# Another fill order with zero products at time zero, conversions in mid-beat, and the reciprocals' row ahead of two loads

## The reference

```python
q, k, v = split(xn @ w_qkv)           # 16 heads of 32
q, k = rope(rmsnorm(q) * gamma_q), rope(rmsnorm(k) * gamma_k)
s = softmax(causal(q @ k.T / sqrt(32))) @ v @ w_out
W = (wq - 128) * scale                 # integer weights, hidden size 1408
g = silu((silu(xn @ Wg.T) * (xn @ Wu.T)) @ Wd.T)
out = x + s * g
```

## Time and profile before

| what | value |
|---|---|
| time, median of 3 runs | 697.89 us (697.45 to 701.13) |
| the profiled execution: its own time, its span | 698.82 us, 697.1 us |
| TensorE busy | 654.9 us, 94% of the span |
| VectorE busy | 540.3 us, 78% |
| ScalarE busy | 456.6 us, 65% |
| GpSimd busy | 413.1 us, 59% |
| DMA moved | 94.40 MB, mean 135 GB/s |

### The profile page before, as it was taken

How to read it: one execution, slowest core, us unless ns; L and a number is a source line. 1 busy time by engine, 2 the same in 40 slices (tenths; PEclk the granted TensorE clock), 3 DMA queues, 4 the chain that set the end, 5 groups by cost and what they waited for, 6 DMA issues and landing times.

```text
span 697.1 us, 12559 instructions
## 1 busy us (share of the span) xinstructions
PE 654.9 (94%) x3690; PEld 552.2 (79%) x3690; DVE 540.3 (78%) x1345; ACT 456.6 (65%) x1010; POOL 413.1 (59%) x590
## 2 busy tenths in 40 slices
PE   5988998999999999899999998999999979969997
PEld 4877887888888888788888887888878866747886
DVE  4795788898787879988878799969786797556584
ACT  2778776787676667876765678766757686633441
POOL 4987676687566657785656678757665583510000
PEclk9999999999999999999999999999999999998999
DMA  7525444414434332144342322244442514479883
GB/s 269 205 106 188 146 154 152 153 36 133 126 104 122 108 96 74 46 138 122 108 123 77 103 78 65 77 132 117 127 137 93 176 52 129 121 219 308 273 318 107
DMA packets 62531, 94.40 MB, mean 135 GB/s; under 512 B 12032, under 2 KB 24320, under 8 KB 62336
## 3 DMA queue, kind: packets, MB, share of 16 engines
q1 hardware_dynamic: 62464, 93.59, 44.0%
HBM read 59.09 MB, written 25.82 MB: 122 GB/s over the span
## 4 chain that ended last, share of the span: by engine, by line
PE 59%; POOL 14%; DVE 8%; issue 7%; DMA 6%; ACT 3%; SPq 2%; DVEq 0%; POOLq 0%; ACTq 0%
PE bank L1405 17%; PE bank L1302 12%; PE bank L1381 7%; PE bank L1342 6%; POOL rr L601 4%; PE bank L1363 4%; PE bank L1431 4%; PE bank L1430 4%; PE bank L1327 3%; PE bank L1314 3%; POOL pp L621 3%; POOL rb L610 2%; POOL ra L607 2%; DMA wd_raw<-w_down 2%; DVE pp L1028 2%
## 5 line engine op out<-in xcount | busy, mean ns | idle before, releaser
L621 POOL TENSOR_SCALAR_AFFINE_SELECT pp<-pp 128x256 fp32r<-128x256 f32 x256 | 110.2, 443 | 145.5 <-DVE pp L1028 145.2
L1050 DVE CUSTOM_DVE_ANT_0 bank<-bank,msk_w 128x128 f32<-128x128 f32 (+3 forms) x256 | 121.1, 509 | 39.3 <-PE bank L1363 39.1
L1028 DVE TENSOR_TENSOR pp<-pf,pp 128x512 fp32r<-128x512 f32 (+1 forms) x192 | 134.8, 702 | 5.8 <-ACT pp L750 5.6
L601 POOL TENSOR_TENSOR rr<-ss,half 128x8 f32<-128x8 f32 x64 | 108.4, 1695 | 24.8 <-DVE ss L996 24.6
L1302 PE MATMUL bank<-wq,xnt_h 128*128 128x384 f32 x512 | 111.9, 340 | 7.2 <-DVE qn L1008 6.8
L749 ACT ACTIVATE pf<-bank 128x512 f32<-128x512 f32 (+1 forms) x192 | 100.6, 524 | 25.6 <-PE bank L1327 23.0
L1405 PE MATMUL bank<-xnt_h,wgu 128*128 128x512 f32 x352 | 98.7, 402 | 7.5 <-DVE g L1078 4.9
L1342 PE MATMUL bank<-pp,va 128*65 128x512 f32 (+3 forms) x512 | 98.1, 310 | 3.3 <-POOL pp L621 3.3
L750 ACT ACTIVATE pp<-bank 128x512 fp32r<-128x512 f32 (+1 forms) x192 | 101.0, 526 | 0.0
L1302 PEld LDWEIGHTS bank<-wq,xnt_h 128*128 128x128 f32 x512 | 88.5, 188 | 11.2 <-issue 8.9
L1405 PE MATMUL bank<-xnt_l,wgu 128*128 128x512 f32 x352 | 96.5, 396 | 0.0
(11 more groups left out here) (83 smaller groups left out, 1187.2 us busy)
## 6 DMA issues: line engine op xcount, KB each, us to landing
wgu<-wg_dram SPq DMA_DIRECT2D x66, 256.0 KB, 3.1
hf_dram<-g SPq DMA_DIRECT2D x44, 256.0 KB, 3.3
hf_raw<-hf_dram SPq DMA_DIRECT2D x16, 512.0 KB, 6.8
wg_dram<-wgu SPq DMA_DIRECT2D x22, 256.0 KB, 3.2
xr<-x SPq DMA_DIRECT2D x16, 256.0 KB, 4.3
oh<-oraw SPq DMA_DIRECT2D x64, 64.0 KB, 2.0
ol<-oraw SPq DMA_DIRECT2D x64, 64.0 KB, 2.0
rdb<-rd_dram SPq DMA_DIRECT2D x16, 256.0 KB
```

The lines of the kernel that those rows point to most:

```text
L601: pool.tensor_tensor(rr[:, s, :], ss[:, s, :], half[:], ALU.pow).then_inc(rr_ok, 1)
L621: op = pool.affine_select(pp[:, :, a:a + P], pp[:, :, a:a + P], [[0, 2], [1, P]], ALU.is_ge, 0.0, base=0, channel_multiplier=-1)
L1028: dve.tensor_tensor(pl[:, tile], pf[:, tile], ph[:, tile].bitcast(F32), ALU.subtract).then_inc(pl_ok, 1)
L1050: op = dve.tensor_tensor_reduce(bank[:, a * w:(a + 1) * w], bank[:, a * w:(a + 1) * w], msk_w[:, N - w:N], 1.0, -3.0e38, ALU.add, ALU.max, ...
```

## The change

The first twelve warm-up products no longer wait for the identity (the wait moves behind them). All five fills get another order; half of the first group's low part goes to GpSimd, and two of the third group's low parts leave the fill for beat 0, so that the later ones move back by a beat. The output weights are converted in four pieces in beats 1 to 4 instead of in one in beat 0. In a beat, the two gate/up conversions for the next beat go from its end to either side of the tanh, and VectorE's product of an odd half goes ahead of the low copy. The down weights' conversion stands one beat later behind its load. In the ending, the broadcast row of reciprocals is issued behind one hidden load instead of three, two hidden loads and a conversion move to an earlier beat, and the orders of ScalarE and VectorE are rewritten to match. Four tiles change their order in memory (`rdb` and `on` now stand ahead of `oh` and `ol`). The diff, cut to its core:

```diff
@@ -192,7 +192,7 @@
-w_hi, w_lo, w_lp = sem("w_hi"), sem("w_lo"), sem("w_lp")
+w_hi, wo_hi, w_lo, w_lp = sem("w_hi"), sem("wo_hi"), sem("w_lo"), sem("w_lp")
@@ -229,16 +229,16 @@
-WARM = (12, 8)
-LATE_W = {0: ((G - 1, 0), (G - 1, 1)), 1: ((G - 1, 2), (G - 1, 3)), 2: ((G, 0),), 3: ((G, 1),), 4: ((G, 2),),
-          5: ((G, 3),)}
+WARM = (12, 0, 8)
+LATE_W = {0: ((2, 2), (2, 3)), 1: ((3, 0), (3, 1)), 2: ((3, 2), (3, 3)), 3: ((G, 0),), 4: ((G, 1),), 5: ((G, 2),),
+          6: ((G, 3),)}
...
-           61: (6,), 62: (7,), 63: (8,)}
-SPLIT_HF = {54: (0,), 55: (1,), 56: (2,), 59: (3,), 60: (4,), 61: (5,), 63: (6,)}
+           61: (6, 7), 62: (8,)}
+SPLIT_HF = {54: (0,), 55: (1,), 56: (2,), 59: (3,), 60: (4,), 61: (5,), 63: (6, 7)}
...
-LATE_SPLIT = {2: (9, 10), 3: (11,)}
+LATE_SPLIT = {}
@@ -403,6 +403,8 @@
+        if i == 0:
+            sp.wait_ge(w_lp, 2 + KT)
@@ -429,7 +431,7 @@
-            sp.wait_ge(w_lp, 5)
+            sp.wait_ge(w_lp, 2)
@@ -498,8 +500,8 @@
         hidden_store(1)
+        first_batch(3)
         m0_out(0, 3, 0)
-        first_batch(3)
 
@@ -521,9 +523,10 @@
     den_in(LAST)
-    for v in range(9, 12):
-        load_hf(v)
+    load_hf(9)
     den_back(LAST)
+    load_hf(10)
+    load_hf(11)
     for t in range(TB):
@@ -577,7 +580,10 @@
-        pool.wait_ge(w_hi, g + 1)
+        if g < G:
+            pool.wait_ge(w_hi, g + 1)
+        else:
+            pool.wait_ge(wo_hi, k + 1)
@@ -662,27 +668,26 @@
         first_rstd(1)
         pool.wait_ge(id_in, 16)
         pool.tensor_copy(idr[:], idf[:]).then_inc(idr_ok, 1)
+        w_low(0, 2, 2)
         first_rstd(2)
+        first_rstd(3)
         tables()
-        first_rstd(3)
         inv_rms(0, 0)
+        inv_rms(1, 1)
+        rope(0, 0, 0)
         gate_scales()
-        rope(0, 0, 0)
-        inv_rms(1, 1)
+        inv_rms(2, 0)
+        rope(1, 1, 1)
         w_low(1, 2, 2)
-        rope(1, 1, 1)
-        inv_rms(2, 0)
+        rope(2, 0, 2)
         inv_rms(3, 1)
-        rope(2, 0, 2)
         rope(3, 1, 3)
         inv_rms(4, 0)
         rope(4, 0, 0)
         inv_rms(5, 1)
+        rope(5, 1, 1)
         w_low(2, 0)
-        rope(5, 1, 1)
         w_low(2, 1)
-        w_low(2, 2)
-        w_low(2, 3)
 
     fill()
     run_beats(pool, beat)
@@ -694,8 +699,11 @@
-        hi = wq[:, g, 0] if g < G else wo_h[:]
-        act.activation(hi.rearrange("p k n -> p (k n)"), staged(g), ACT.Copy).then_inc(w_hi, 1)
+        act.activation(wq[:, g, 0].rearrange("p k n -> p (k n)"), staged(g), ACT.Copy).then_inc(w_hi, 1)
+
+    def split_wo(k):
+        act.wait_ge(w_in[G], 16)
+        act.activation(wo_h[:, k, :], staged(G, k, 1), ACT.Copy).then_inc(wo_hi, 1)
@@ -828,7 +836,7 @@
-            act.wait_ge(w_lp, 1)
+            act.wait_ge(w_lp, 2)
@@ -857,11 +865,13 @@
 
-            act.wait_ge(w_lp, 5 + 2 * KT)
+            act.wait_ge(w_lp, 2 + 3 * KT)
         if k == 0 and (c - 8) // 4 % 4 != G - 1 and there(4 * r + (c - 8) // 4, B * G):
...
         o_out()
+        gu_weights(half_at(c + 1, 0))
         gate(half_at(c, 0))
+        gu_weights(half_at(c + 1, 1))
         if not s_on:
@@ -876,10 +886,8 @@
             o_high(4 * r + (c - 7) // 4, G - 1)
-        gu_weights(half_at(c + 1, 0))
-        gu_weights(half_at(c + 1, 1))
-        if c == 0:
-            split_w(G)
+        if 1 <= c <= KT:
+            split_wo(c - 1)
         for v in SPLIT_HF.get(c, ()):
@@ -897,57 +905,60 @@
 
     def fill():
         xt_high(0, 0)
+        xt_high(0, 1)
         split_w(0)
-        xt_high(0, 1)
         first_square(0)
         xt_high(0, 2)
+        first_square(1)
+        xt_high(0, 3)
         split_w(1)
         gu_weights(0)
-        xt_high(0, 3)
-        first_square(1)
+        first_square(2)
         gu_weights(1)
+        gu_weights(2)
         t_high(0, 0)
-        gu_weights(2)
-        first_square(2)
+        gate(0)
+        first_square(3)
         turned(0)
-        first_square(3)
-        split_w(2)
         t_high(1, 1)
-        gate(0)
-        first_square(4)
         turned_k(0)
         turned(1)
+        first_square(4)
         t_high(2, 0)
         turned_k(1)
-        t_high(3, 1)
         turned(2)
         first_square(5)
+        t_high(3, 1)
         turned_k(2)
+        gate(2)
         gu_weights(3)
         turned(3)
+        t_high(4, 0)
         gu_weights(4)
         turned_k(3)
-        t_high(4, 0)
+        split_w(2)
+        turned(4)
+        first_square(6)
+        turned_k(4)
         split_w(3)
-        turned(4)
-        gate(2)
-        turned_k(4)
-        first_square(6)
         gu_weights(5)
 
     fill()
     run_beats(act, beat)
 
     outer(0, 0)
-    high(7)
     high(8)
     outer(0, 1)
-    for n in range(2, B * TB):
+    high(9)
+    o_high(LAST, G - 1)
+    high(10)
+    outer(0, 2)
+    high(11)
+    outer(0, 3)
+    for n in range(4, B * TB):
         b, t = divmod(n, TB)
         for v in LATE_SPLIT.get(n, ()):
             high(v)
-        if n == 3:
-            o_high(LAST, G - 1)
         outer(b, t)
         if TB < n <= 2 * TB:
             s_evac(B - 1, n - TB - 1, LATE_PS[n - TB - 1])
@@ -1094,11 +1105,15 @@
             squares(j + 6, (c + 6) % 2)
+        up = half_at(c - 1, 1) is not None and half_at(c - 1, 1) % 2
+        if up:
+            gated(half_at(c - 1, 1))
         if there(j + 5, NB):
...
             v_low(j + 6, (c + 6) // 4 % VR, (c + 6) % 4)
-        gated(half_at(c - 1, 1))
+        if not up:
+            gated(half_at(c - 1, 1))
         if k != 3:
@@ -1141,8 +1156,8 @@
             ln_apply(b, t)
-        if c - 1 in LOAD_WD:
-            wd_weights(LOAD_WD[c - 1])
+        if c - 2 in LOAD_WD:
+            wd_weights(LOAD_WD[c - 2])
         for v in SPLIT_HF.get(c, ()) if c > 56 else ():
@@ -1152,61 +1167,61 @@
     def fill():
         dve.memset(pp[:, 0, 0:N].bitcast(F32), 0.0).then_inc(zero_ok, 1)
         ln_stats(0, 0)
+        ln_stats(0, 1)
         ln_apply(0, 0)
-        ln_stats(0, 1)
         ln_apply(0, 1)
         xt_low(0, 0)
+        xt_low(0, 1)
         ln_stats(0, 2)
-        w_low(0, KT)
-        xt_low(0, 1)
+        ln_stats(0, 3)
+        w_low(0, 2)
         ln_apply(0, 2)
-        ln_stats(0, 3)
+        ln_apply(0, 3)
         squares(0, 0)
-        ln_apply(0, 3)
+        xt_low(0, 2)
+        squares(1, 1)
+        xt_low(0, 3)
+        unit_rms(0, 0)
+        unit_rms(1, 1)
         first_v(0)
-        xt_low(0, 2)
-        unit_rms(0, 0)
-        xt_low(0, 3)
-        squares(1, 1)
+        squares(2, 0)
+        rope_sum(0, 0)
         first_v(1)
-        rope_sum(0, 0)
         t_low(0, 0)
-        unit_rms(1, 1)
+        gated(0)
+        unit_rms(2, 0)
+        first_v(2)
+        rope_sum(1, 1)
         w_low(1, 2)
-        first_v(2)
-        squares(2, 0)
+        t_low(1, 1)
+        squares(3, 1)
         first_v(3)
-        squares(3, 1)
-        rope_sum(1, 1)
-        unit_rms(2, 0)
-        t_low(1, 1)
-        gated(0)
+        maxima(0, 0, (0,))
...
@@ -1234,18 +1249,24 @@
     scaled(0, 0)
     scaled(0, 1)
     recip(LAST)
-    low(7)
     low(8)
-    for n in range(2, B * TB):
+    low(9)
+    scaled(0, 2)
+    o_low(LAST, G - 1)
+    low(10)
+    scaled(0, 3)
+    finish(0, 0)
+    finish(0, 1)
+    low(11)
+    scaled(1, 0)
+    finish(0, 2)
+    finish(0, 3)
+    for n in range(TB + 1, B * TB):
         b, t = divmod(n, TB)
         for v in LATE_SPLIT.get(n, ()):
             low(v)
         scaled(b, t)
-        if n == 2:
-            finish(0, 0)
         finish(*divmod(n - 1, TB))
-        if n == 3:
-            o_low(LAST, G - 1)
     scaled(B - 1, TB - 1, 1)
     finish(B - 1, TB - 1)
     finish(B - 1, TB - 1, 1)
@@ -1253,8 +1274,6 @@
-    pe.wait_ge(id_in, 16)
-
@@ -1274,7 +1293,7 @@
-        wait(pe, w_lp, (0, 1, 5, 9)[g])
+        wait(pe, w_lp, (1, 2, 6, 10)[g])
@@ -1531,49 +1550,51 @@
 
     def fill():
         warm(WARM[0])
+        pe.wait_ge(id_in, 16)
         xn_turn(0, 0, 0)
+        warm(WARM[1])
         xn_turn(0, 0, 1)
-        warm(WARM[1])
+        warm(WARM[2])
         project(0, 0, 0)
+        project(0, 1, 0)
         project(0, 0, 1)
         xn_turn(0, 0, 2)
-        project(0, 1, 0)
+        project(0, 1, 1)
         xn_turn(0, 0, 3)
-        project(0, 1, 1)
         project(0, 2, 0)
+        project(0, 2, 1)
         project(0, 3, 0)
-        project(0, 2, 1)
+        gate_half(0)
         project(0, 3, 1)
         pe.wait_ge(idr_ok, 1)
         turn(0, 0, 0)
         project(0, 4, 0)
-        gate_half(0)
+        project(0, 5, 0)
         turn(0, 0, 1)
         project(0, 4, 1)
-        project(0, 5, 0)
+        maxima(0, 0, (0,))
         turn(0, 1, 0)
-        maxima(0, 0, (0,))
         gate_half(1)
         turn(0, 1, 1)
         project(0, 5, 1)
+        turn(0, 2, 0)
         maxima(0, 1, (0,))
-        turn(0, 2, 0)
         maxima(0, 1, (1,))
         turn(0, 2, 1)
+        gate_half(2)
+        maxima(0, 2, (0,))
+        maxima(0, 2, (1,))
```

(62 more changed lines are left out.)

## The result

The changed kernel takes 692.63 us (four runs, 690.49 to 696.00) against 698.44: ratio 0.9919, 95% interval 0.9892 to 0.9946, some 5.7 us less. On a second chip it came out at 0.9889 (0.9867 to 0.9911), 7.8 us. The forecast was 17.0 less (680.9, range 676.5 to 687.5): the sign is right, the size is a third to under a half of it, and the time lies outside the range.

The account below looks back on a forecast made before the run. TensorE, busy 94% of the span, was taken as the bound, so gains come from its idle time. Head and fill 5.3, beats 3.7, down weights 2.4 and ending 5.6 sum to 17.0 us: 697.89 to 680.9, range 676.5 to 687.5.

Parts of the forecast that it names:

- Head: Start of TensorE: first projection at 10.2 instead of 14.46, 4.3 us earlier, bound by the landing of the weights.
- Fill: From first projection to the beats: first scores at 43.3, a gain of 5.3 us for head and fill together.
- Between 6.8 and 3.8 I take 43.3: Fill: first scores placed between a TensorE-bound start (gain 6.8 us) and a GpSimd-bound one (3.8); gain taken 5.3.
- rival C: Fill: GpSimd or the maxima bind it, gain 2 of 5.3 us, time 684; chance 0.15.
- Beats 0 to 8: First batch: gate-product waits summing to 5.0 us end, less conversion delays; net gain 3.7 us, bounds 1.0 and 5.0.
- issue and use move forward together: Beats 0 to 7: argument against late integers, that their loads move forward with the conversions using them.
- rival E: Beats 0 to 7: ScalarE's conversions wait for their integers, deciding from 2.1 us a beat; at 3, 705 us; chance 0.03.
- Down weights: Beats 45 to 55: with a beat more to land, both TensorE waits go, 2.4 us; bounds 0 and 2.4.
- Ending: Last output projections: earlier row of reciprocals and full clock give 6.7 us, less 1.1, net 5.6; bounds 0 and 7.5.
- I take 6.6, near the first: Ending: row of reciprocals lands 6.6 us after issue, at 622.3, near the earlier 6.4 rather than 9.5.
- 1.4: Ending: TensorE restarts at 624.4 instead of 629.00, 1.4 us behind the end of its own work.
- the clock should hold: Ending: after the shorter gap TensorE keeps full clock, twelve products taking 2.75 instead of 4.90 us, worth 2.1.

Follow-up runs that it names:

- b_fill: The kernel before with the change's head and fill alone; ratio to the kernel before 0.9975, 1.7 us less.
- spint: The changed kernel with SP's integer stores and loads of beat 6 issued in beat 5, ahead of the gather; 684.78 us, ratio to the kernel before 0.9800.
- b_wd: The kernel before with only the down weights converted a beat later; ratio to the kernel before 0.9976, 1.7 us less.
- b_four: The kernel before with only the broadcast row of reciprocals issued as four transfers, one a head; 692.27 us, ratio to the kernel before 0.9891.
- b_end: The kernel before with only the change's ending (hidden loads, row of reciprocals, new orders); ratio to the kernel before 0.9956, 3.1 us less.
- hold: The changed kernel with nothing issued behind the row of reciprocals until it has landed; ratio to the kernel before 0.9902.
- four: The changed kernel with the broadcast row of reciprocals issued as four transfers, one a head; 686.51 us, ratio to the kernel before 0.9799.
- hi7: The changed kernel with hidden conversion 7 and its low part back in their old places in the ending; 691.70 us, ratio to the kernel before 0.9871.

## Why the prediction was wrong, step by step

1. *Head: right in its place, too large in its size.* 10.2 was forecast, 10.61 came (10.1 to 10.9 in all profiles with it). But 14.46 was the latest of its kind: in five other profiles in which TensorE waits for the identity first, the first projection starts at 11.7 to 13.2. The start of one execution carried 1.3 to 2.8 of the 4.3 us, of which 1.2 to 2.1 is the identity's landing (6.71 against 4.58 to 5.53).
2. *Fill: failed.* "Between 6.8 and 3.8 I take 43.3", with fewer pauses. From the first projection to the first scores it took 34.3 in four where the clock held (34.15 in the earlier trace rows), and 35.7 to 35.8 in four where it fell. GpSimd's first root came at 16.35 (15.7 forecast), but its last three ropes waited 4.9 for normalised rows (3.4 where the clock held), against some 1.2 forecast. In the eight profiles of this order it took 26.3 to 26.4 from the first root to the end of the sixth rope where the clock held and 27.8 where it fell, and not 24.8. First scores: 44.4 to 46.6 (median of eleven 44.9) against 46.6 to 48.6 (of six 47.4), 2.5 and not 5.3, and by the ratio of b_fill 1.7. This is nearest to rival C, with the waits on VectorE in place of GpSimd's own work; the fall of the clock, 1.5 us in five profiles of eleven, was in no term.
3. *Beats 0 to 8: failed, and the largest miss.* The term was 3.7 less; the stretch took 3.4 more. The step that failed is "issue and use move forward together", given against rival E: the use moved 9.0 us forward and the issue 4.1, since SP was held at a gather. The trace before had the sign: ScalarE waited 1.29 for this very load at 115.86, issued behind the same gather, and the L1078 wait of 1.51 behind it was booked among those that the new order ends. The forecast looked for E in every beat, at 2.1 us a beat; it came in one, at 6.4, with half clock behind it. With SP's place mended spint has the 3.7.
4. *Down weights: right*, 2.6 in place in b_wd, 1.9 and 2.2 in the change. b_four shows that the row in four transfers would have done as much.
5. *Ending: mechanism right, somewhat too large.* 5.6 was forecast, b_end as a whole gives 3.1; from beat 60 to the end four profiles with the old ending and one row take 109.9, 109.9, 110.4 and 111.0 (b_fill 112.3), nine with the new one 104.4 to 108.1, median 105.6. The profiled execution of the change is the longest of the nine. Two terms were off. "I take 6.6, near the first": from issue to product the row took 6.3 to 9.0 in eight profiles behind one load, because what is issued behind it counts too (hold, four). The gap of "1.4" does not follow from its own rows either: 624.4 is 0.9 behind 623.5, where TensorE's work ended (629.00 - 5.46); it measured 2.55, and 1.59 in the other execution. And "the clock should hold": in the profiled execution there are two gaps of 2.5, with 4.58 us for the twelve products of the earlier trace rows; the second gap, on the scaled result, was not in the forecast. It goes when the pair of conversion 7 moves back (hi7), with another wait in its place and no gain, and with the pair where it is when the row goes as four transfers (0.17 in four). The row's issue, 615.48 against 615.53, is no earlier, though all before it was.

By place, won against forecast: 2.5 against 5.3, -3.4 against 3.7, 1.9 to 2.6 against 2.4, 3 to 5 against 5.6. The single parts as measured (1.7, -2.5, 1.7, 3.1) sum to 4.0, each uncertain by 1.1 to 1.3, together by 2.4; the whole gave 5.7 and 7.8. What is left between the sum and 7.8 stays open.

## What to carry to other kernels

Before moving a use forward, find the issue of its data in the issuing engine's queue and read what that queue waits for there: the same lead can be short in one beat and ample in all others. Where several profiles of one order can be had, take a landing from all of them. A broadcast that is late may be cheaper to reshape than to reorder: here four transfers in place of one brought as much as the whole change.
